# GpSimd's work in pieces of 128 columns, and a new order for norms, context and late loads, in a transformer block on one core

## What is computed

```python
def rms_norm(x, scale, eps=1e-6):
    ms = jnp.mean(jnp.square(x), axis=-1, keepdims=True)
    return x * jax.lax.rsqrt(ms + eps) * scale

q = rms_norm(x @ q_w + q_b, nq_s).reshape(B, S, H, D)
k_img = rms_norm(img_ctx @ ki_w + ki_b, nki_s).reshape(B, -1, H, D)
v_img = (img_ctx @ vi_w + vi_b).reshape(B, -1, H, D)
out = (out_txt + sdpa(q, k_img, v_img)).reshape(B, S, INNER)
...
x = x + tanh(g_xattn[0]) * _L0_xattn_ref(_layernorm(x), ctx, ...)
x = x + tanh(g_ffn[0])   * _L0_ffn_ref(_layernorm(x), ...)
x = x + tanh(g_xattn[1]) * _L1_xattn_ref(_layernorm(x), ctx, ctx)
x = x + tanh(g_ffn[1])   * _L1_ffn_ref(_layernorm(x), ...)
```

## Time and profile before

| | us |
|---|---|
| three runs | 1387.26, 1389.5, 1400.32 |
| median | 1389.5 |
| profiled execution, its own time | 1393.94 |
| its span in the profile | 1392.2 |
| mean granted TensorE clock over the span | 0.976 of full speed |

### The profile page before, as it was taken

One profiled execution on the slowest core, in us unless ns is written; L12 is line 12 of the kernel. 1 busy time (PEld: TensorE's weight loads), 2 busy tenths in 40 slices (PEclk: granted clock), 3 DMA queues, 4 the chain that ended last, 5 costly groups with the idle time before them and its releaser, 6 DMA issues.

```text
span 1392.2 us, 26516 instructions
## 1 busy us (share of the span) xinstructions
PE 1281.2 (92%) x9929; PEld 1120.3 (80%) x9929; DVE 861.7 (62%) x2180; ACT 806.6 (58%) x2177; POOL 496.9 (36%) x465
## 2 busy tenths in 40 slices
PE   7898998999898998989989899898989999788898
PEld 6677897888788987888779888798878998787686
DVE  4446548774575646766466655757566564677575
ACT  5556776656644666456655566546764566555622
POOL 2444452534334343344423344234433445100000
PEclk9899999999999999999999999999999999889999
DMA  8543364423432333323442343332433242212201
GB/s 290 218 167 137 142 221 152 137 92 122 152 121 92 122 128 130 122 90 125 146 141 91 121 137 119 125 122 91 137 137 121 77 137 92 91 61 79 89 1 46
DMA packets 51692, 171.37 MB, mean 123 GB/s; under 512 B 4592, under 2 KB 23280, under 8 KB 43248
## 3 DMA queue, kind: packets, MB, share of 16 engines
q1 hardware_dynamic: 51568, 169.69, 35.3%
HBM read 148.70 MB, written 20.97 MB: 122 GB/s over the span
## 4 chain that ended last, share of the span: by engine, by line
PE 79%; DVE 10%; ACT 5%; issue 4%; SPq 1%; DMA 1%; POOL 0%; POOLq 0%; ACTq 0%; DVEq 0%
PE bank L118 56%; PE bank L1089 8%; PE bank L1100 4%; PE bank L1210 2%; PE bank L1222 2%; PE bank L1078 2%; ACT logit L827 1%; DVE rstd L82 1%; ACT xn L863 1%; PE bank L1254 1%; PE bank L1164 1%; PE bank L1362 1%; DVE ntmp L81 1%; DVE ao_lo L1583 1%; PE bank L1061 1%
## 5 line engine op out<-in xcount | busy, mean ns | idle before, releaser
L705 POOL TENSOR_TENSOR k_sq<-k_sb 128x512 f32<-128x512 f32 x120 | 126.5, 1054 | 356.2 <-ACT k_sb L840 356.2
L716 POOL TENSOR_TENSOR q_sum<-q_sum,q_sq 128x512 f32<-128x512 f32 x105 | 137.5, 1309 | 279.3 <-ACT q_sq L857 278.7
L118 PE MATMUL bank<-ct_hi,wqk 128*128 128x512 f32 x512 | 193.5, 420 | 14.7 <-issue 10.3
L118 PE MATMUL bank<-so,ao_hi 128*128 128x256 f32 x1008 | 200.8, 297 | 1.5 <-DVE ao_lo L1583 1.5
L118 PE MATMUL bank<-sv,ct_hi 128*128 128x256 f32 x1024 | 198.4, 292 | 0.0
L118 PE MATMUL bank<-xt_hi,wqk 128*128 128x512 f32 x512 | 185.9, 405 | 10.4 <-ACT k_sb L840 9.6
L827 ACT ACTIVATE logit<-logit,least 128x64 f32<-128x64 f32 x512 | 171.1, 341 | 41.8 <-DVE least L1595 41.8
L1583 DVE SCALAR_TENSOR_TENSOR ao_lo<-bank,vecs,ao_hi 128x512 fp32r<-128x512 f32 x126 | 94.5, 750 | 142.4 <-ACT ao_hi L821 141.9
L1089 PEld LDWEIGHTS bank<-pt,v_sb 128*128 128x128 f32 x1024 | 134.6, 195 | 44.1 <-issue 36.3
L118 PEld LDWEIGHTS bank<-sv,ct_hi 128*128 128x128 f32 x1024 | 161.6, 192 | 10.0 <-issue 7.3
L118 PEld LDWEIGHTS bank<-so,ao_hi 128*128 128x128 f32 x1008 | 159.4, 195 | 10.0 <-issue 9.9
(11 more groups left out here) (218 smaller groups left out, 2743.6 us busy)
## 6 DMA issues: line engine op xcount, KB each, us to landing
wqk<-qk_scratch SPq DMA_DIRECT2D x56, 1024.0 KB, 6.1
sv<-v_scratch SPq DMA_DIRECT2D x56, 512.0 KB, 3.3
so<-o_scratch SPq DMA_DIRECT2D x56, 512.0 KB, 3.3
qk_scratch<-wqk SPq DMA_DIRECT2D x8, 1024.0 KB, 4.0
xin<-in_x_dram SPq DMA_DIRECT2D x8, 512.0 KB, 6.7
cs<-in_ctx_turned_dram SPq DMA_DIRECT2D x8, 512.0 KB, 7.1
xres<-in_x_dram SPq DMA_DIRECT2D x8, 512.0 KB, 7.7
v_scratch<-sv SPq DMA_DIRECT2D x8, 512.0 KB, 2.6
```

Source lines behind the costliest of these rows:

```text
L118: last = pe.matmul(out, lhs[a], rhs[b], start=start and n == 0, stop=stop and n == 2, **kw)
L705: pool.tensor_tensor(k_sq[:, h % 2, :] if h else total[0], k_sb[:, h % 4, :], k_sb[:, h % 4, :], ALU.mult).then_inc(k_squared.sem, 1)
L716: pool.tensor_tensor(total[1], total[1], q_sq[:, h % 2, :], ALU.add).then_inc(q_added.sem, 1)
```

## The change

GpSimd's sums and squares of k, the two biases and the context sum are cut into operations of 128 columns, and q's squares are added by VectorE in all bodies (before: in the prologue alone). The output bias moves from step 14 to behind step 15. `norms` moves from point "d" to point "e" of step 0, behind the output product; `mean_squares` follows to step 1, point "a". The Newton steps are split: the guess and one step stay at step 1, point "b", the other two, `rr` and the first `logits` come behind `prob_copy` of step 1. The context is split by halves: ScalarE's first half at the end of step 14, the second where the whole stood; VectorE's first half at the start of step 15, the second where the whole stood. In the prologue the tokens of group 1 are loaded before the first store of split weights and their statistics are taken in step 5, not in step 1; the V weights, the context of group 1, `oraw` and the residual move behind the stores of the split K and Q weights. `WEIGHT_ORDER` is written in another way and has the same value; the signals are renamed to fit.

```diff
+PIECE = P
@@ SyncE
         def load_turned(g):
-            split_lo.wait(sp, g - 1, 0)
+            context_lo.wait(sp, g - 1, 1)
...
         load_weights("q", 1)
+        load_inputs(1)
         keep_weights(0)
         keep_weights(1)
-        load_inputs(1)
-        load_value_weights(0)
-        load_value_weights(1)
...
-        load_residual(0)
-        sp.dma_start(oraw[:, :, :], o_w.rearrange("(h p) d -> p h d", h=H)).then_inc(s_oraw, 16)
-        load_turned(1)
         for h in range(1, H, 2):
             if h + 3 < H:
                 keep_weights((h + 3) // 2)
             else:
                 fetch_weights(0, h)
+            if h == 1:
+                load_value_weights(0)
+            if h == 3:
+                load_turned(1)
+            if h == 5:
+                load_value_weights(1)
+            if h == 9:
+                sp.dma_start(oraw[:, :, :], o_w.rearrange("(h p) d -> p h d", h=H)).then_inc(s_oraw, 16)
+            if h == 11:
+                load_residual(0)
@@ GpSimd
+        def in_pieces(out, a, b, op):
+            for at in range(0, GT, PIECE):
+                piece = slice(at, at + PIECE)
+                last = pool.tensor_tensor(out[:, piece], a[:, piece], b[:, piece], op)
+            return last
...
-                pool.tensor_tensor(total[0], total[0], k_sq[:, h % 2, :], ALU.add).then_inc(k_added.sem, 1)
-            if h and g:
-                pool.wait_ge(q_squared.sem, q_squared.count(g, h))
...
-                pool.tensor_tensor(total[1], total[1], q_sq[:, h % 2, :], ALU.add).then_inc(q_added.sem, 1)
+                in_pieces(total, total, k_sq[:, h % 2, :], ALU.add).then_inc(k_added.sem, 1)
...
             for t in range(NT):
-                last = pool.tensor_tensor(xres[:, t, :], xres[:, t, :], bias0[:, :], ALU.add)
+                for c in range(DC):
+                    part = slice(c * P, (c + 1) * P)
+                    last = pool.tensor_tensor(xres[:, t, part], xres[:, t, part], bias0[:, part], ALU.add)
...
-                if b >= 0 and h == 14:
-                    with_output_bias(b)
                 if b + 1 < NG:
                     add_squares(b + 1, h)
+            if b >= 0:
+                with_output_bias(b)
@@ ScalarE
             if final:
-                split_context(b + 2)
+                split_context(b + 2, 1)
...
+            if h == H - 2 and b + 2 < NG:
+                split_context(b + 2, 0)
@@ TensorE
-            if "F" in parts and at == (0, "d"):
+            if "F" in parts and at == (0, "e"):
                 norms(b)
@@ VectorE
-                if at == (1, "a"):
+                if at == ((1, "a") if b >= 0 else (5, "b")):
                     tile_stats(n)
...
-                if at == (0, "e"):
+                if at == (1, "a"):
                     mean_squares(b)
                 if at == (1, "b"):
-                    score_factors(b)
+                    score_guess(b)
...
+            if h == H - 1 and b + 2 < NG:
+                split_context(b + 2, 0)
...
-            if live(b, h - 1):
+            if live(b, h - 1) and h != 1:
                 logits(b, h - 1)
...
             if h == H - 1 and b + 2 < NG:
-                split(b + 2, 0)
+                split_context(b + 2, 1)
+            if h == 1 and live(b, 0):
+                score_factors(b)
+                logits(b, 0)
             share(b, h, "d")
+            if 0 <= b < NG - 1 and h:
+                add_squares(b + 1, h)
             share(b, h, "e")
```

More of the change, by code:

```diff
@@ L106 @@
 FIRST_K = 4
-WEIGHT_ORDER = [(n, p) for p in range(2) for n in ("k", "q")] + [(n, p) for p in range(2, PAIRS) for n in "kq"]
-WEIGHT_ORDER[1], WEIGHT_ORDER[2] = WEIGHT_ORDER[2], WEIGHT_ORDER[1]
+WEIGHT_ORDER = [("k", 0), ("k", 1), ("q", 0), ("q", 1)] + [(n, p) for p in range(2, PAIRS) for n in "kq"]
+PIECE = P
 PARTS = (slice(0, FIRST_HEADS * HD), slice(FIRST_HEADS * HD, INNER))
@@ L720, in with_output_bias @@
             for t in range(NT):
-                last = pool.tensor_tensor(xres[:, t, :], xres[:, t, :], obias[:, :], ALU.add)
+                for c in range(DC):
+                    part = slice(c * P, (c + 1) * P)
+                    last = pool.tensor_tensor(xres[:, t, part], xres[:, t, part], obias[:, part], ALU.add)
             last.then_inc(xres_ready.sem, 1)
@@ L737, in with_context_sum @@
             for t in range(NT):
-                x = tokens(s)[:, t, :]
-                last = pool.tensor_tensor(x, x, csum[:, t:t + 1].to_broadcast([P, D]), ALU.add)
+                for c in range(DC):
+                    x = tokens(s)[:, t, c * P:(c + 1) * P]
+                    last = pool.tensor_tensor(x, x, csum[:, t:t + 1].to_broadcast([P, P]), ALU.add)
             last.then_inc(x2c_ready.sem, 1)
@@ L1269, in transposes @@
                 pe.wait_ge(xn_ready.sem, xn_ready.count(g, 0))
-                split_lo.wait(pe, g - 1, 1)
+                tokens_lo.wait(pe, g - 1, 0)
             turned(g, "tr", j, xin, tr_full)
@@ L1549, in first_context @@
         def first_context():
-            dve.wait_ge(split_hi.sem, split_hi.count(0, 1))
-            dve.tensor_tensor(context[0][1][:, :, :], cs[:, :, :], context[0][0][:, :, :].bitcast(F32),
-                              ALU.subtract).then_inc(split_lo.sem, 1)
+            for c in range(DC):
+                dve.wait_ge(context_hi.sem, context_hi.count(0, c))
+                dve.tensor_tensor(context[0][1][:, c, :], cs[:, c, :], context[0][0][:, c, :].bitcast(F32),
+                                  ALU.subtract).then_inc(context_lo.sem, 1)
         def first_tokens(j):
@@ L1558, in first_tokens, with add_squares, split_context, split_tokens @@
             if j == 1:
-                last.then_inc(split_lo.sem, 1)
-        def add_first_squares(h):
-            dve.wait_ge(q_squared.sem, q_squared.count(0, h))
+                last.then_inc(tokens_lo.sem, 1)
+        def add_squares(g, h):
+            dve.wait_ge(q_squared.sem, q_squared.count(g, h))
             if h > 1:
-                dve.wait_ge(q_added.sem, q_added.count(0, h - 2))
-            dve.tensor_tensor(q_sum[:, 0, :], q_sum[:, 0, :], q_sq[:, h % 2, :], ALU.add).then_inc(q_added.sem, 1)
-        def split(g, n):
-            lo, hi, src = ((context[g % 2][1], context[g % 2][0], cs), (xt_lo, xt_hi, xs))[n]
-            dve.wait_ge(split_hi.sem, split_hi.count(g, n))
-            dve.tensor_tensor(lo[:, :, :], src[:, :, :], hi[:, :, :].bitcast(F32),
-                              ALU.subtract).then_inc(split_lo.sem, 1)
+                dve.wait_ge(q_added.sem, q_added.count(g, h - 2))
+            total = q_sum[:, g % 2, :]
+            dve.tensor_tensor(total, total, q_sq[:, h % 2, :], ALU.add).then_inc(q_added.sem, 1)
+        def split_context(g, half):
+            hi, lo = [feature_major(v, half) for v in context[g % 2]]
+            dve.wait_ge(context_hi.sem, context_hi.count(g, half))
+            dve.tensor_tensor(lo, feature_major(cs, half), hi.bitcast(F32), ALU.subtract).then_inc(context_lo.sem, 1)
+        def split_tokens(g):
+            dve.wait_ge(tokens_hi.sem, tokens_hi.count(g - 1, 0))
+            dve.tensor_tensor(xt_lo[:, :, :], xs[:, :, :], xt_hi[:, :, :].bitcast(F32),
+                              ALU.subtract).then_inc(tokens_lo.sem, 1)
         def prob_copy(g, h):
```

42 lines of the change are left out of this document (23 added, 19 removed).

## The result

The changed kernel takes 1333.9 us (median of four runs, 1332.7 to 1335.1), the kernel before 1389.2; the ratio is 0.9586 with a 95% interval from 0.9535 to 0.9637. The forecast was 1351 and its range 1330 to 1380: faster as said and inside the range, but 60.1 us less between the profiled executions (1393.94 and 1333.81), where the sum had 38.9. Between the medians it is 55.3 us: the profiled execution of before was 4.7 us above its median. (The text and the shortened diff above put the load of group 1's tokens ahead of the first store of split weights; in the kernel it stands between the two first stores.)

The account below looks back on a forecast made before the run. TensorE, busy 92% of the span, bounds the kernel, so only its gaps can close. Prologue 14 + body 0 3.5 + bodies 1 to 6 19 + body 7 2.4 = 38.9 off 1393.9, less 4.4: 1351 us, range 1330 to 1380.

Parts of the forecast that it names:

- the likeliest case's own range: Whole kernel: 1336 to 1364 us if the forecast case (chance 0.56) holds, with the additions' charge between 0 and 4.
- Prologue: New load order removes TensorE's pauses of 5.69 and 4.33 us and the low clock behind them: 14 us, bounds 7 and 16.
- Body 0: First body: 2.2 us of the 5.17 wait and 1.3 of its first k product, 3.5 in all, bounds 0 and 6.
- The gains in a body: Bodies 1 to 6, each: k projection 1.2 us, norms and Newton steps 2.4, step 6 2.1, before charges.
- The new wait forecast at the q product of step 2: In a body, TensorE would newly wait 0.7 us there for `k_sb`; already subtracted in the norms' net 2.4.
- ScalarE's charge of 0.4 a body for the halves: End of step 14: ScalarE's one more operation for the halved context split costs 0.4 us, bounds 0 and 0.62.
- The charge for the additions: q's squares on VectorE: hidden except in dense steps 2, 9 and 15, costing 2.1 us a body, bounds 0 and 10.4.
- The clock: Prologue only: stretches at granted clock 0.50 and 0.60 behind the pauses lose 2.5 and 1.7 us, both to go.
- Body 7: Last body, without splits or additions: gains only the 2.4 us of the norms.
- VectorE as the bound: Rival, chance 0.07: all 105 additions cost 0.69 us each on the path, making the kernel slower at 1445 us.
- the bodies gain nothing: Rival, chance 0.24: holds return as often as they shorten; only prologue, body 0 and last norms gain 19.9, giving 1369.6 us.
- Late loads: Rival, chance 0.13: loads moved behind the stores delay weights TensorE needs, 9.4 us of the prologue's gain goes: 1360 us.

Follow-up runs that it names:

- run 4: The changed kernel with the prologue's old order of loads and the statistics of group 1 at step 1 again: 1347.7 us, ratio 0.9654.
- run 8: The kernel before with only the prologue's new order of loads and the statistics of group 1 at step 5: 1378.0 us, ratio 0.9889.
- run 6: The changed kernel with both halves of the context's split back at the old place of the whole, on ScalarE and VectorE: 1338.5 us, ratio 0.9590.
- run 7: The kernel before with only GpSimd's operations cut into pieces of 128 columns, q's sums among them: 1377.4 us, ratio 0.9877.
- run 1: The changed kernel with GpSimd's operations whole again (512 and 256 columns): 1352.8 us, ratio 0.9692.
- run 5: The changed kernel with norms at point d, mean squares at step 0 and unsplit Newton steps ahead of the probabilities: 1358.2 us, ratio 0.9729.
- run 2: The changed kernel with q's sums of groups 1 to 7 back on GpSimd, in pieces of 128: 1347.8 us, ratio 0.9654.
- run 3: The changed kernel with the 105 additions of q's squares on VectorE cut from 512 to 8 columns: 1335.6 us, ratio 0.9571.
- run 12: The changed kernel with GpSimd's squares, sums and biases in operations of 256 columns, not 128: 1341.1 us, ratio 0.9647.

## Why the prediction was right, and where its sum failed

The direction and the causes held. The size did not: the gain between the profiled executions is some 21 us above the sum, and 1333.9 lies below 1336, the end of the likeliest case's own range. That it lies inside the whole range, by 4 us, is in part luck: the low end stands there by larger gains in the prologue and body 0 and by bodies without charges, not by the clock that made much of the difference. By its steps:

- *Prologue: 14 forecast, 10.9 measured,* confirmed from both sides (runs 4 and 8). Both pauses went. Part of the rest was given back in a place that the step did not name: the statistics of group 1, moved to step 5, make its transposes in step 7 late, and TensorE waits 2.60 there (1.39 before) and runs at 0.66 behind it:

```profile
46.72 0.69 PE L1182 MATMUL bank<-ident,xin 128*128 128x128 f32 x2 [2.60 <-ACT xin L805]
```
```profile
46.60:51.60 5.00, 4.88 (x45) 4.15 (x46) 2.91 (x4) 3.47 (x8) 4.21 (x8) 0.66 0.57 234
```

- *Body 0: 3.5 forecast, 4.6 measured.* Its wait at the q product fell from 5.17 to 3.12, about as counted. The first k product, for which 1.3 was counted, still waits 1.64 (1.80 before); part of the 4.6 is clock (0.97 to 0.99).
- *The gains in a body, 1.2 + 2.4 + 2.1 = 5.7 forecast:* the right size, not always by the cause named. Before the first k product 1.23 went, but the pieces are enough for it without the halves' new places (runs 6 and 7); in run 1, with whole operations and the halves apart, only some 0.26 is left of it as well. The norms went from 2.52 to 1.10 and `attend` from 1.57 to nothing; the prediction put the second down to the order, and with the old order only 0.41 of it returns (run 5): most went with the shorter holds. Step 6 went from 2.87 to 1.41, 1.5 where 2.1 was forecast, and not under the 1 us that was to be seen there; body 6 has no such wait before or after. The new wait forecast at the q product of step 2, 0.7 and ended by `k_sb`, is 1.57 in body 1 and is not listed in bodies 2 to 6; run 2, with q's sums on GpSimd, has it at 0.71. A wait of 0.74 at the q product of step 6, which the prediction had not looked at, went as well. ScalarE's charge of 0.4 a body for the halves is what run 6 measures.
- *The charge for the additions, 2.1 a body: this term failed.* It was charged "in full" in three steps. Run 3 puts the additions at nothing (0.2), and run 2 shows that their move gains 1.7 a body, since VectorE's operations meet fewer of GpSimd's. The sign of the term was wrong. It was 12.6 of the six bodies' sum, and without it the six bodies' sum is 31.8 us. They gave 39.2, of which 9.8 are clock (next step): some 29.
- *The clock: counted in the prologue alone, 4.2, where 22.7 was to be had; this term was too small.* Bodies 1, 2 and 4 stood at 0.97 and 0.98 before and 1.00 after, body 3 at 1.00 and 0.99: 0.02 x 151.3 + 0.03 x 168.7 + 0.02 x 167.0 - 0.01 x 159.8 = 9.8 of these bodies' 39.2 us. Body 7 stood at 0.94 and 0.97.
- *Body 7: 2.4 forecast for its norms, 6.0 measured,* and this is no more than the clock (0.06 x 199.7 - 0.03 x 193.7 = 6.2). Of the waits, the norms' fell from 2.25 to 0.82, and that at `attend`, 3.91, came back as 4.54 at the transposes of `prob`: the late `logits` of head 0, which the prediction named as its lower bound, cost here what they saved. With the old order (run 5) the 3.91 is back and the 4.54 gone.

The rivals: VectorE as the bound is out (run 3). That the bodies gain nothing is out (4.0 to 5.7 us in bodies at full clock). The Trainium skill, "Perfetto Trace Analysis", section "Optimizing Scalar/DVE Operations", says that moving operations between GpSimd and VectorE might not help. Here it did: moving 105 additions from GpSimd to VectorE was worth 14 us (run 2). Late loads do not come too late: the list of TensorE's waits has none that ends with a load.

Whether a wait makes the clock fall is only partly settled, and with it why the clock gave back as much as it did. The same wait of 2.52 at the norms was followed by two different clocks in the execution of before, in body 2 and in body 3:

```profile
380.30:388.00 7.70, 7.62 (x28) 6.43 (x29) 2.82 (x9) 0.58 (x4) 0.00 (x0) 0.56 0.10 20
549.00:554.00 5.00, 4.98 (x32) 4.26 (x32) 2.82 (x9) 0.66 (x5) 0.00 (x0) 1.00 0.11 38
```

In run 5 it fell behind that wait five times of five, in the changed kernel, behind a norms' wait of 1.10, once in bodies 2 to 6. In these traces longer waits go with more stretches of low clock, but they do not say when one comes.

## What to carry to other kernels

An engine that is off the critical path can still be the one to change: count not its busy time but how long each of its operations can hold another engine, and how often. Cut such operations small, and move work to the engine that is held if it has idle time in the right places. Where work is moved later in an order, look also at the stages with the least other work: a wait that is covered in the full bodies can come back there, as in body 7. And look for the wait's second price: behind a wait of TensorE read the granted clock, and put what it costs into the sum of every stage, not only of the worst.

## What the runs showed of the hardware

- A VectorE operation with two inputs in memory is held by GpSimd even if it has four columns: 0.16 us alone, 0.38 to 0.44 beside pieces of 128 columns (run 2), 0.91 to 1.15 beside whole ones. In run 2 four such operations in a row were held. So in a chain beside GpSimd's work the number of small operations counts, and not their size alone. The Trainium skill, "SBUF — State Buffer", section "Who interferes with whom", says that such an operation contends with a GpSimd instruction that reads SBUF, and that the loser of the port pair they share is blocked for the whole of the other's instruction. The longest `prob` agrees: 1.507 beside whole operations, 0.907 beside 256 columns (run 12), 0.737 beside 128.
- GpSimd's additions go by a straight line: the sum of k's squares takes 1.292 us for 512 columns, 0.739 for 256 (run 12) and 0.460 for 128, all medians. Cutting a 512-column sum in four makes it 0.5 us longer; all the cuts together make the kernel 19 us faster (run 1).
- A body of run 1 is 1.0 us longer at full clock than one of the changed kernel, and the execution 19 us: by the rough measure of the first section 10.9 of these are clock, not waiting.
